# A Perceiver layer on one core: context taken relative to its last token, and the self-attention products in one block between transposes and weighted values

## The reference, cut to what matters

```python
# cross-attention, 16 heads of 16, no mask; x: (128, 32, 256), ctx: (128, 257, 256)
q = split(norm(x) @ Wq.T + bq); k = split(ctx @ Wk.T + bk); v = split(ctx @ Wv.T + bv)
x1 = x + softmax(q @ k.T) @ v @ Wo.T + bo
# self-attention over the 32 rows of a sequence, rotary, sigmoid weights divided by their sum
y = norm(x1)
q, k = rope(rms(y) @ q_w.T + q_b), rope(rms(y) @ k_w.T + k_b)
w = sigmoid(q @ k.T / 4); w = w / (w.sum(-1) + 1e-8)
x2 = x1 + (w @ (y @ v_w.T + v_b)) @ o_w.T + o_b
# top-1 of 8 experts with a capacity of 160 rows each, in the order of the tokens
p = softmax(norm(x2) @ gate_w + gate_b); e = argmax(p); keep = rank_within_expert < 160
out = x2 + keep * p[e] * (gelu(norm(x2) @ w1[e] + b1[e]) @ w2[e] + b2[e])
```

## Time and profile before

| | |
|---|---|
| three runs | 1315.08, 1319.5, 1319.97 us; median 1319.5 us |
| the profiled execution | 1326.77 us, its span 1324.9 us |
| mean granted clock of TensorE | 0.946 |
| busy in the span | TensorE 88%, its weight loads 74%, VectorE 64%, ScalarE 61%, GpSimd 43% |
| tiles with all stages | from about 120 to 1140 us |

### The profile page before, as it was taken

The page is one execution under the profiler, slowest core; times in us unless marked ns, Lnnn a source line. Parts: engine busy times, 40 slices in busy tenths (PEclk is TensorE's granted clock), DMA queues, the critical chain, the costliest instruction groups (busy, mean ns, idle before and its releaser), DMA issues. The chain is left out here.

```text
span 1324.9 us, 43348 instructions
## 1 busy us (share of the span) xinstructions
PE 1160.6 (88%) x17169; PEld 980.9 (74%) x17169; DVE 851.6 (64%) x2395; ACT 801.9 (61%) x2347; POOL 568.9 (43%) x1045
## 2 busy tenths in 40 slices
PE   6898988989889889999988988998999988874897
PEld 5677777777777777777777777777787777752796
DVE  4667777776776677766677766777666667653111
ACT  5677666666666666666666766766656666632121
POOL 2344444454554444445445444444444544432021
PEclk9999999998999999989999999999888999975899
DMA  6415111111111111111111111111111111000474
GB/s 156 124 46 182 54 58 54 58 57 34 52 50 54 49 36 50 51 47 52 36 47 48 50 51 31 50 50 51 46 45 36 48 50 46 14 10 13 135 227 138
DMA packets 71927, 82.32 MB, mean 62 GB/s; under 512 B 16987, under 2 KB 50732, under 8 KB 71728
## 3 DMA queue, kind: packets, MB, share of 16 engines
q1 hardware_dynamic: 65280, 75.19, 19.3%
q0 software_dynamic: 3200, 3.71, 0.8%
q10 hardware_dynamic: 3248, 0.66, 0.2%
HBM read 64.79 MB, written 16.56 MB: 61 GB/s over the span
## 5 line engine op out<-in xcount | busy, mean ns | idle before, releaser
L735 ACT ACTIVATE prob<-score,nmx 128x257 f32<-128x257 f32 x512 | 236.2, 476 | 219.1 <-DVE nmx L936 218.8
L401 PE MATMUL kps<-ctx_p,wk_p 128*128 128x256 f32 x1536 | 217.4, 292 | 0.3 <-POOL ctx_p L1235 0.2
L411 PE MATMUL vps<-wv_p,ctx_p 128*128 128x256 f32 x1536 | 214.7, 289 | 0.0
L401 PEld LDWEIGHTS kps<-ctx_p,wk_p 128*128 128x128 f32 x1536 | 200.0, 196 | 6.1 <-issue 1.9
L1235 POOL TENSOR_TENSOR ctx_p<-ctxT,ctx_p 128x512 fp32r<-128x512 f32 x128 | 152.3, 1190 | 117.1 <-ACT ctx_p L751 116.7
L411 PEld LDWEIGHTS vps<-wv_p,ctx_p 128*128 128x128 f32 x1536 | 191.5, 191 | 12.4 <-issue 12.4
L936 DVE TENSOR_REDUCE nmx<-score 128x2 f32<-128x514 f32 x256 | 165.2, 687 | 51.7 <-PE score L428 51.7
L1253 POOL TENSOR_TENSOR plast<-const,prob 128x128 f32<-128x128 f32 x128 | 64.1, 501 | 255.8 <-DVE prob L947 255.8
L947 DVE TENSOR_SCALAR prob<-prob,rsum 128x257 f32<-128x257 f32 x512 | 158.5, 352 | 9.0
L953 DVE COPY probT<-score 128x512 f32<-128x512 f32 x96 | 66.4, 691 | 126.2 <-PE score L444 125.9
L444 PE MATMUL score<-const,prob 128*128 128x128 f32 x1024 | 140.8, 281 | 2.3 <-DVE prob L947 2.1
(11 more groups left out here) (159 smaller groups left out, 2029.3 us busy)
## 6 DMA issues: line engine op xcount, KB each, us to landing
ctxT<-in_ctxT SPq DMA_DIRECT2D x128, 257.0 KB, 3.0
w<-in_w SPq DMA_DIRECT2D x16, 1024.0 KB, 8.7
xq<-in_x SPq DMA_DIRECT2D x32, 128.0 KB, 3.2
xr<-in_x SPq DMA_DIRECT2D x32, 128.0 KB, 2.1
qbd<-qkT SPq DMA_DIRECT2D x256, 16.0 KB, 1.9
out<-row SPq DMA_DIRECT2D x32, 128.0 KB, 1.9
slots<-row SPq DMA_DIRECT2D x10, 257.0 KB, 5.6
x_a<-slots SPq DMA_DIRECT2D x8, 129.0 KB, 2.1
```

Source lines behind the costliest of these rows:

```text
L401: last = mm(kps[:, c, :], wk_p[:, x, n, c * P:(c + 1) * P], ctx_p[:, g, y, n, :], start=(n, x) == (0, LO), stop=(n, y) == (C - 1, LO))
L411: last = mm(vps[:, c, :], ctx_p[:, g, x, n, c * P:(c + 1) * P], wv_p[:, y, n, :], start=(n, x) == (0, LO), stop=(n, y) == (C - 1, LO))
L735: last = af(prob[:, m, :], score[:, m, 0:S], ACT.Exp, bias=nmx[:, m:m + 1], scale=1.0, accum_out=esum[:, m:m + 1])
```

## The change

- **Relative context.** From every context token its sequence's last token is subtracted (`nlast` is the negated last token). Within a softmax a shift common to all keys cancels, so the last key is just the bias `b_k`, set once in `kT`; since the weights sum to one, the values relative to the last value give the result when the last value is added, which `extract` does from `vlast`. `last_key`, `last_prob`, `last_probs`, `attended`, `alast`, `plast` and `klast` go, and `normalise` covers 256 columns.
- **The parts of the context.** `context_hi` becomes two instructions of 128x256 with a bias, earlier in the slot. `context_lo` moves from GpSimd to VectorE, two instructions a slot with three inputs. The parts of y1 move too: high part on ScalarE (`rows_hi`), low part on VectorE (`rows_lo`), straight from PSUM. Both rope products are VectorE's.
- **The order.** The table `between` is another, and with it the order of the small works on VectorE, ScalarE, GpSimd and the loads of `xq` on SyncE. `choose` and `gate_exp` run one tile later. `self_values` moves from behind the values (1, 2) to behind the transposes (1, 3), all 16 heads in one block. The gate's transposes go to a bank of the scores (`spare2_c`), the positions too.

The core of the diff:

```diff
-            def last_probs(t):
...
-            def project_out(x, w, ready, t, done):
-                pe.wait_ge(s[ready], t + 1)
+            def project_out(x, w, ready, count, t, done):
+                pe.wait_ge(s[ready], count)
...
-                    (0, 0): s1 and (lambda: (turn("att_tmp", t1 + 1), last_probs(t1))),
-                    (0, 1): lambda: (t3 is not None and positions(t3),
-                                     s2 and (turn("relu_done", t2 + 1), scores2(t2))),
...
-                    (1, 2): s2 and (lambda: (turn("att2n_done", t2 + 1), self_values(t2))),
...
+                    (0, 0): s2 and (lambda: (turn("relu_done", t2 + 1), scores2(t2))),
...
+                    (1, 3): s2 and (lambda: self_values(t2, range(H))),
...
             def context_hi(t, j):
                 b, r, g = TB * t + j, j // 2, j % 2
+
                 act.wait_ge(ctx_in[r], 16 * C * (t + 1))
                 act.wait_ge(s["v_done"], floor0(b - 1))
-                af(ctx_p[:, g, HI, :, :], ctxT[:, r, :, g, 0:SM], ACT.Copy).then_inc(s["ctx_hi"], 1)
+                for c in range(C):
+                    last = af(ctx_p[:, g, HI, c, :], ctxT[:, r, c, g, 0:SM], ACT.Identity, bias=nlast[:, c, b:b + 1], scale=1.0)
+                last.then_inc(s["ctx_hi"], 1)
...
+            def context_lo(t, j):
+                b, r, g = TB * t + j, j // 2, j % 2
+                dve.wait_ge(s["ctx_hi"], b + 1)
+                for c in range(C):
+                    last = v.scalar_tensor_tensor(ctx_p[:, g, LO, c, :], ctxT[:, r, c, g, 0:SM], nlast[:, c, b:b + 1],
+                                                  ctx_p[:, g, HI, c, :].bitcast(F32), ALU.add, ALU.subtract)
+                last.then_inc(s["ctx_parts"], 1)
...
-                        last = v.tensor_scalar(prob[:, m, :], prob[:, m, :], rsum[:, m:m + 1], None, ALU.mult)
+                        last = v.tensor_scalar(prob[:, m, 0:SM], prob[:, m, 0:SM], rsum[:, m:m + 1], None, ALU.mult)
...
+                v.scalar_tensor_tensor(att[:, :, :].rearrange("p c (j q) -> p c j q", j=TB),
+                                       gather[:, :, 0, :].rearrange("p c (j q) -> p c j q", j=TB), k["even"],
+                                       vlast[:, t, :, :].unsqueeze(3).to_broadcast([P, C, TB, L]), ALU.mult, ALU.add
+                                       ).then_inc(s["ext_step"], 1)
...
+            def rows_lo(t):
+                dve.wait_ge(s["y1T_hi"], t + 1)
+                v.tensor_tensor(y1T_p[:, LO], spare_c, y1T_p[:, HI].bitcast(F32), ALU.subtract).then_inc(s["y1T_parts"], 1)
```

More of the change, by code:

```diff
@@ new lines, in body @@
+                if xa:
+                    maxima(i, 0)
+                    context_lo(i, 2)
+                if s1:
+                    extract(t1)
+                if once(i):
+                    norm_x(1)
+                if xa:
+                    normalise(i, 0)
+                if i >= 3:
+                    choose(t2 - 1)
+                if xa:
+                    probsT(i, 0)
+                if q:
+                    norm_x_apply(i + 1)
+                if s1:
+                    residual1(t1)
@@ new lines, in body @@
+                if s1:
+                    residual1_stats(t1)
+                    residual1_mean(t1)
+                if once(i):
+                    last_values()
+                if s2:
+                    sigmoid_product(t2)
+                if xa:
+                    maxima(i, 1)
+                if s1:
+                    norm1(t1)
+                if xa:
+                    context_lo(i, 3)
+                if xa:
+                    normalise(i, 1)
+                if xa:
+                    probsT(i, 1)
@@ new lines, in body @@
+                if i >= 3:
+                    position(t2 - 1)
+                if s1:
+                    rows_lo(t1)
+                if s2:
+                    inverse2(t2)
+                    weigh2(t2)
+                if xa:
+                    maxima(i, 2)
+                if s1:
+                    evac_qk(t1)
+                if xa:
+                    normalise(i, 2)
+                if s1:
+                    rope_products(t1)
+                if q:
+                    context_lo(i + 1, 0)
@@ new lines, in body @@
+                if s1:
+                    rope_add(t1)
+                if once(i):
+                    setup_scales()
+                if s2:
+                    residual2(t2)
+                if xa:
+                    maxima(i, 3)
+                if s2:
+                    residual2_stats(t2)
+                    residual2_mean(t2)
+                if q:
+                    context_lo(i + 1, 1)
+                if s2:
+                    norm2(t2)
+                if xa:
+                    normalise(i, 3)
+                    probsT(i, 3)
```

343 lines of the change are left out of this document (121 added, 222 removed).

## The result

The changed kernel takes **1232.28 us** (median of 4 runs, 1230.05 to 1238.1), the kernel before beside it 1319.74 us: ratio 0.9355, with a 95% interval of 0.9309 to 0.9401. It is faster, and by 87 us where I had forecast 39. The time lies inside the range, the effect is more than twice the forecast. The profiled execution took 1232.15 us, with a span of 1229.9 us.

A forecast was written before the change was run, and what follows sets the result against it. TensorE sets the pace, VectorE nearly level after the change. 1.42 us a tile saved, net 1.2 after the clock, gives 35 us over 29 tiles; with 4 us at the ends, 39 us off: 1281 us, range 1226 to 1318.

The forecast's parts named there:

- main mechanism: Slot 0, TensorE: without the last key's product and the wait for `alast`, 8.1 us against 10.85.
- the 257th key: Slot 0, TensorE: the last key's waits and product were said to cost about 3.3 us.
- The prices of `context_lo`, of the rope products and of slots 2 and 3: VectorE: 0.9 us a context_lo pair, about 0.42 us a rope product; TensorE: slot 2 7.75 us, slot 3 8.85.
- I leave that as it is: Slot 1, TensorE: the 64 small self-attention products keep about 2.5 us a tile after their move.
- Waits 1.7 us: Slot 1: VectorE late, halves normalised at 5.2 and 6.0 us, TensorE out of work at about 4.1; length 9.65 us.
- waits smaller than counted: Rival, TensorE's slots: half of the 3.85 us of waits goes, gain 3.1 us a tile, 1226 us; chance 0.25.
- the low clock I expect in nearly every tile: TensorE, after slot 1's late transposes, self-attention and weighted values in one run: about 1.0 us a tile instead of 0.80.
- GpSimd didn't hold VectorE: Rival, new VectorE subtractions: each context_lo pair waits for GpSimd, 3.0 us a tile, 1368 us; chance 0.10.
- `scores2` never waited for `qbd2`: Rival, scores2 in slot 0: `qbd2` transfers one microsecond late, gain only 0.2 us a tile, 1310 us; chance 0.08.

The follow-up runs named there:

- the run with the old order: Changed kernel with TensorE's slot 0 ordered as before (scores2 behind the keys, project_out behind the values): 1245.19 us.
- The context_lo made twice: Changed kernel with each pair of context_lo done a second time, into a tile that nothing reads: 1294.9 us.
- the later extraction: Changed kernel with VectorE's two extraction operations behind the normalisation of slot 0 instead of ahead of it: 1233.09 us.
- a version where they meet: Changed kernel with self-attention in two halves, plus context_lo for slot 2 ahead of the maxima of slot 0 on VectorE: 1183.3 us.
- third set: Runs on one chip, including the changed kernel unaltered at 1231.7 us beside the kernel before, unaltered, at 1277.16 us.
- a third part: Changed kernel with self-attention in parts of 5, 5 and 6 heads, early context_lo and ScalarE's y2T ahead of its values in slot 3: 1173.37 us.

## Why the prediction was right or wrong

- **Direction and main mechanism: right.** Slot 0 lost 3.0 us (10.85 to 7.82, forecast 2.75). By the run with the old order 0.43 of them are the order's; 2.6 are left for the 257th key and what else went from the slot. The prices of `context_lo`, of the rope products and of slots 2 and 3 hold within 0.1 us.
- **The step that failed first: "I leave that as it is".** The self-attention block was kept at 2.5 us although put 27.9 us of its time down to issue, in a place that the change dissolved. It measured 1.19 us: 1.31 us a tile. The block's move alone took 1.37 us off the tile but only 0.67 off the block, which took 1.81 then; the other 0.62 came only together with the rest of the change.
- **The second: "Waits 1.7 us" in slot 1.** The halves were to come 5.2 us after the scores; the transposes start 4.6 after them. With the block that is the whole 1.93 us. I had read right that VectorE is late there. The context_lo made twice shows slots 0 and 1 bound by it, and the later extraction costs nothing there. I only made it 0.6 us too late: I had the maxima of slot 1 start 1.8 us after its scores, and they start 1.41 after. This is the mechanism of the rival "waits smaller than counted" (1226 us), with a second cause beside it.
- **The third: "the low clock I expect in nearly every tile".** It fell in seven stretches of the full tiles. What comes on top of the undisturbed step is 33.40 less 32.03, 1.37 us a tile, where I had 1.0; but it is of another kind, pauses in the supply of instructions in groups of tiles, with the clock behind them. I had read the low clock as a matter of what the tile holds. In every trace here it fell in the full tiles only in or right behind a stretch in which TensorE stood idle: in the kernel before the two stops in the block (0.36 and 0.50 us), in the changed kernel the pauses, with context_lo made twice also the wait of 1.05 us for VectorE. Not every such stretch brought it: six of the thirteen pauses of the changed kernel did not.
- **The sum.** 2.32 us less in the undisturbed tile (0.28, 1.93, 0.10 and 0.01 by slots) less 0.37 us more disturbance, over 29 tiles, are 57 us. The profiled gain is 94.6 us against 39 forecast, 56 more.
- **The rivals.** GpSimd didn't hold VectorE in the changed order (0.87 us a pair); in a version where they meet it did, by 0.48 us. `scores2` never waited for `qbd2`.
- **What no reading of the one profile could tell**: in two of the four sets the kernel before takes 1277 to 1278 us, and beside it the change is worth 45 us (third set, ratio 0.9625) and not 87. Of these 42 us, 0.84 us a tile are the pauses in the block (35.77 against 34.93), about 26 us. The remainder I put down to the clock, fifteen stretches against none; no run shows it alone. Each of the four sets was made on another chip and at another time, so which of the two makes the difference is not shown.

Open stays why the kernel before pauses longer in its block in some sets than in others. It isn't the stream's fixed place, as these pauses lie in nearly every tile at the same product (46 and 51 loads into the block). Open is also what the block's move alone gives where there are no pauses.

## What to carry to other kernels

A block whose time is largely "issue" is not of fixed length: price it both as it stands and as one full run. Where a dense run of small products stands counts too: the same 64, moved whole from behind the transposes to behind the values, made this kernel 28 us faster, in halves 35, and a third part took 8 more off although the undisturbed tile in halves was shorter. A pause named "issue" whose place moves evenly from tile to tile is found by counting the instructions up to it. And before an engine's own order is tuned, double one of its operations: the slots that grow are those which it bounds.

## What the hardware did that I had not expected

- A pause of 1.2 to 2.1 us in TensorE's stream at thirteen of 117 places 256 instructions apart, where these fall into or behind the dense part of slot 1, each ending 1.2 to 1.6 us after a packet of instructions landed; in the undisturbed tiles between the same places pass without one.
- The same program at 1277, 1320 and 1330 us in different sets, while the changed one took 1232.28 us beside 1319.74 and 1231.7 beside 1277.16.
- The clock was granted lower behind a pause of 1.35 us (0.66 in 660 to 665 us), and behind a wait of 1.05 us for VectorE in the run with context_lo twice; in no full tile of any trace did it fall without an idle stretch of TensorE at it or just before.
- Products of 32x17 follow each other with their weight loads at 9.3 ns (1.19 us for 128 records) where the block runs through.
